# Query projections computed in row halves beside the gate and up products, and placed ahead of the weight folds

## The reference, cut to what matters

```python
xn = layernorm(x)
q  = xn @ Wq;  k, v = split(xn @ Wkv)
s  = softmax_causal(q @ k.T / 4) @ v @ Wo + bo
gate = xn @ gate_w.T + (xn @ gate_a.T) @ gate_b.T      # rank 16
up   = xn @ up_w.T   + (xn @ up_a.T) @ up_b.T
hidden = silu(gate) * up                                # 1376 wide
y = hidden @ down_w.T + (hidden @ down_a.T) @ down_b.T
out = x + s * silu(y)
```

## Time and profile before

| | |
|---|---|
| median of 3 runs | 969.41 us (967.91 to 973.47) |
| the profiled execution | 968.28 us, its span 966.6 us |
| granted clock of TensorE, mean | 0.98 |
| PE busy | 902.3 us, 93% of the span |
| DVE busy | 580.3 us, 60% |
| ACT busy | 490.9 us, 51% |
| POOL busy | 318.7 us, 33% |

### The profile page before, as it was taken

One profiled execution on the slowest core, in us unless ns is written; L12 is line 12 of the kernel. 1 busy time (PEld: TensorE's weight loads), 2 busy tenths in 40 slices (PEclk: granted clock), 3 DMA queues, 4 the chain that ended last, 5 costly groups with the idle time before them and its releaser, 6 DMA issues.

```text
span 966.6 us, 21098 instructions
## 1 busy us (share of the span) xinstructions
PE 902.3 (93%) x8075; PEld 633.4 (66%) x8075; DVE 580.3 (60%) x1681; ACT 490.9 (51%) x990; POOL 318.7 (33%) x320
## 2 busy tenths in 40 slices
PE   2797999999999999999999999998999999999996
PEld 2665666666666666767576666554777777777774
DVE  6755666666666666565756575767666667621134
ACT  2433555556565555555656565656454544545110
POOL 4022225252525252525252434441122213211036
PEclk8899999999999999999999999999899999999998
DMA  9466243333334242424243434347556566335644
GB/s 297 130 196 191 82 116 104 115 107 104 117 92 129 83 138 67 149 56 140 71 135 86 118 103 118 98 140 226 154 151 173 147 184 173 110 94 166 193 133 159
DMA packets 142946, 129.20 MB, mean 134 GB/s; under 512 B 36176, under 2 KB 104368, under 8 KB 142624
## 3 DMA queue, kind: packets, MB, share of 16 engines
q1 hardware_dynamic: 142848, 127.87, 44.6%
HBM read 74.07 MB, written 53.22 MB: 132 GB/s over the span
## 4 chain that ended last, share of the span: by engine, by line
PE 79%; DVE 8%; DMA 6%; ACT 2%; SPq 2%; issue 2%; POOL 0%; POOLq 0%; DVEq 0%; ACTq 0%
PE bank L965 25%; PE o L1134 12%; PE bank L999 12%; PE s L1098 9%; PE st L1117 7%; PE bank L267 3%; PE bank L269 2%; PE bank L268 2%; DVE junk L1624 2%; DVE neg_pad L1640 1%; PE bank L940 1%; PE bank L944 1%; DMA q<-scratch_q 1%; DVE hid L1489 1%; SPq L648 1%
## 5 line engine op out<-in xcount | busy, mean ns | idle before, releaser
L1380 ACT ACTIVATE prob<-st 128x512 f32<-128x512 f32 (+1 forms) x640 | 323.1, 554 | 258.4 <-PE st L1117 257.9
L1624 DVE CUSTOM_DVE_ANT_0 junk<-s,mask 128x128 bf16<-128x128 f32 (+3 forms) x512 | 229.3, 487 | 114.0 <-PE s L1098 113.4
L1627 DVE TENSOR_REDUCE part_max<-s 128x1 f32<-128x512 f32 x256 | 163.8, 681 | 97.0 <-PE s L1098 96.9
L1098 PE MATMUL s<-k,q 64*128 64x512 f32 (+3 forms) x768 | 150.9, 380 | 14.4 <-DVE part_max L1624 9.9
L533 POOL TENSOR_SCALAR_AFFINE_SELECT prob<-prob 128x512 f32<-128x512 f32 x128 | 82.7, 658 | 223.1 <-ACT prob L1380 222.6
L965 PE MATMUL bank<-x_hi,w_hi 64*128 64x512 f32 (+1 forms) x704 | 150.5, 415 | 2.4 <-DVE hid L1489 1.1
L1134 PE MATMUL o<-prob,v 128*32 128x512 f32 (+3 forms) x1536 | 143.7, 492 | 0.0
L965 PE MATMUL bank<-x_lo,w_hi 64*128 64x512 f32 (+1 forms) x704 | 142.6, 392 | 0.0
L965 PE MATMUL bank<-x_hi,w_lo 64*128 64x512 f32 (+1 forms) x704 | 141.6, 389 | 0.0
L1117 PE MATMUL st<-q,k 64*128 64x512 f32 (+3 forms) x768 | 130.0, 355 | 1.9 <-ACT prob L1380 1.8
L999 PE MATMUL bank<-down_hi,hid_in 64*128 64x256 f32 x1056 | 114.1, 289 | 0.3 <-DVE y L1505 0.3
(11 more groups left out here) (138 smaller groups left out, 1092.1 us busy)
## 6 DMA issues: line engine op xcount, KB each, us to landing
hid_in<-scratch_hid SPq DMA_DIRECT2D x16, 1408.0 KB, 7.1
q<-scratch_q SPq DMA_DIRECT2D x60, 200.0 KB
scratch_hid<-tanh_hid_hi SPq DMA_DIRECT2D x40, 256.0 KB, 2.1
scratch_hid<-hid_lo SPq DMA_DIRECT2D x40, 256.0 KB, 2.5
scratch_o<-o_sb SPq DMA_DIRECT2D x32, 256.0 KB
scratch_q<-proj_hi SPq DMA_DIRECT2D x30, 256.0 KB
k<-scratch_k SPq DMA_DIRECT2D x30, 192.0 KB
ctx<-scratch_o SPq DMA_DIRECT2D x16, 256.0 KB, 3.8
```

Of the source, the lines that this page charges most:

```text
L1098: pe.matmul(sb_[(p + odd) % S_BANKS][:, 0:wd], q[half, g % 2, h // 2, qt * P:(qt + 1) * P], k[half, g % 2, k0:k0 + wd], start=True, stop=T ...
L1380: nc.scalar.activation(prob[:, job % 3, h, 0:JOB_COLS[j]], st[at % ST_BANKS][:, 0:JOB_COLS[j]], ACT.Exp, scale=float(HD) ** -0.5).then_inc ...
L1624: ins = dve.tensor_tensor_reduce(junk[:, n % S_BANKS, 0:wd], bank_[:, 0:wd], mask[:, C - wd:C], 1.0, LOWEST, ALU.add, ALU.max, part[:, h, ...
L1627: ins = dve.tensor_reduce(part[:, h, qt, dst:dst + 1], bank_[:, 0:wd], AX.X, ALU.max)
```

## The change

Eleven of the 16 projections of queries (4 blocks of heads for 4 chunks of tokens), those inside the loop over `h` (`AFTER[1:]`, now `BESIDE_HIDDEN`), are computed by `changing_over` with the steps of the output product. The left 256 tokens of the chunk go to `bank[0]` and the right 256 to `bank[1]`. In the first two steps the upper 64 rows of the array add their part of the left tokens while the lower 64 rows add theirs of the right ones; then both change over. 12 matmuls of 128 rows by 512 columns become 48 of 64 rows by 256 columns. Such a projection takes both banks. ACT and DVE read it in two halves each. A new semaphore `p_left` counts the left half read by DVE, and `p_lo` the right one; whoever takes either bank next waits for both.

The second part is the order. The projection now stands directly behind `hidden(h, 1)` and ahead of the two folds, on all engines.

```diff
+BESIDE_HIDDEN = AFTER[1:]
@@ bank_order (and likewise in the loops of SP, PE, ACT and DVE)
             if c == 1:
+                yield "proj", *AFTER[SOON + h]
                 if h + 1 < NH:
                     for i in range(2):
                         yield "fold", h + 1, i
-                yield "proj", *AFTER[SOON + h]
@@ bank_places
-        if kind == "hidden" or kind == "down" and a < SPLIT_DOWN or kind == "out" and a < SPLIT_OUT:
+        if kind == "hidden" or kind == "proj" and (a, b) in BESIDE_HIDDEN or kind == "down" and a < SPLIT_DOWN or kind == "out" and a < SPLIT_OUT:
             used = (0, 1)
@@ read_out
+            if kind == "proj" and (a, b) in BESIDE_HIDDEN:
+                return (p_left, BESIDE_HIDDEN.index((a, b)) + 1), (p_lo, projection(a, b) + 1)
@@ project
+                if (c, blk) in BESIDE_HIDDEN:
+                    cols = slice(blk * P, (blk + 1) * P)
+                    yield from changing_over(
+                        ("proj", c, blk), lambda kt: [(wqh[:, kt, cols], xh[:, c, kt]), (wqh[:, kt, cols], xl[:, c, kt]),
+                                                      (wql[:, kt, cols], xh[:, c, kt])], OUT_STEPS)
+                    return
@@ split_projection (ACT)
-                nc.scalar.activation(projected(n)[0], bank_of(key)[:, :], ACT.Copy).then_inc(p_hi, 1)
+                if (c, blk) in BESIDE_HIDDEN:
+                    for i in range(2):
+                        ins = nc.scalar.activation(projected(n)[0][:, COLUMNS[i]], bank[i][:, COLUMNS[i]], ACT.Copy)
...
+                ins.then_inc(p_hi, 1)
@@ low_projection (DVE)
+                if (c, blk) in BESIDE_HIDDEN:
+                    for i, read in enumerate((p_left, p_lo)):
+                        dve.tensor_tensor(lo[:, COLUMNS[i]], bank[i][:, COLUMNS[i]], hi[:, COLUMNS[i]], ALU.subtract).then_inc(read, 1)
```

More of the change, by code:

```diff
@@ L396, in layer @@
         p_lo = sem("p_lo")
+        p_left = sem("p_left")
         p_stored = [sem(f"p_stored{i}") for i in range(2)]
@@ L759, in background @@
                         if c == 1:
+                            yield STEPS["proj"]
+                            store_projection(*AFTER[SOON + h])
                             if h + 1 < NH:
@@ L763, in background @@
                                     load_more_raw(2 * (h + 1) + i)
-                            yield STEPS["proj"]
-                            store_projection(*AFTER[SOON + h])
                 for h in range(NH):
@@ L1063, in background @@
                         if c == 1:
+                            yield from project(*AFTER[SOON + h])
                             if h + 1 < NH:
@@ L1066, in background @@
                                     yield from fold(h + 1, i)
-                            yield from project(*AFTER[SOON + h])
                 for h in range(NH):
@@ L1187, in split_projection @@
                     act.wait_ge(p_stored[n % 2], 3 * DMA * (n // 2))
-                nc.scalar.activation(projected(n)[0], bank_of(key)[:, :], ACT.Copy).then_inc(p_hi, 1)
+                if (c, blk) in BESIDE_HIDDEN:
+                    for i in range(2):
+                        ins = nc.scalar.activation(projected(n)[0][:, COLUMNS[i]], bank[i][:, COLUMNS[i]], ACT.Copy)
+                else:
+                    ins = nc.scalar.activation(projected(n)[0], bank_of(key)[:, :], ACT.Copy)
+                ins.then_inc(p_hi, 1)
             def copy_value(c):
@@ L1329, in background @@
                         if c == 1:
+                            yield STEPS["proj"]
+                            split_projection(*AFTER[SOON + h])
                             if h + 1 < NH:
@@ L1333, in background @@
                                     split_weight(h + 1, i)
-                            yield STEPS["proj"]
-                            split_projection(*AFTER[SOON + h])
                 for h in range(NH):
@@ L1456, in low_projection @@
                     dve.wait_ge(zero_stored, DMA * (B + 2))
-                dve.tensor_tensor(lo, bank_of(key)[:, :], hi, ALU.subtract).then_inc(p_lo, 1)
+                if (c, blk) in BESIDE_HIDDEN:
+                    for i, read in enumerate((p_left, p_lo)):
+                        dve.tensor_tensor(lo[:, COLUMNS[i]], bank[i][:, COLUMNS[i]], hi[:, COLUMNS[i]], ALU.subtract).then_inc(read, 1)
+                else:
+                    dve.tensor_tensor(lo, bank_of(key)[:, :], hi, ALU.subtract).then_inc(p_lo, 1)
             def low_of_low(n, part_, raw, at):
@@ L1574, in background @@
                         if c == 1:
+                            yield STEPS["proj"]
+                            low_projection(*AFTER[SOON + h])
                             if h + 1 < NH:
@@ L1578, in background @@
                                     low_weight(h + 1, i)
-                            yield STEPS["proj"]
-                            low_projection(*AFTER[SOON + h])
                 for h in range(NH):
```

## The result

| | before | changed |
|---|---|---|
| median of 12 runs | 970.00 us | 975.85 us |
| range | 967.88 to 973.47 | 973.81 to 977.17 |
| the profiled execution | 968.28 | 973.99 |
| its span | 966.6 | 971.2 |

The ratio is 1.0054 (95% interval 1.0039 to 1.0068): 0.5% slower, on the line between "no change" and "slower" that the prediction had drawn. The forecast was 971.5 and the range 961 to 980. The direction it leaned to was right, the size was less than half of what came. The profiled executions differ by 5.7 us and their spans by 4.6: before, 1.7 us lie around the span, after, 2.8.

The account below looks back on a forecast made before the run. PE was taken as the bound. A block: -1.09 + 1.21 + 0.20 = +0.32, ten blocks +3.2, the eleventh projection -0.6, together +2.6 on the profiled 968.28; forecast 971.5 us, range 961 to 980.

Parts of the forecast that it names:

- PE bounds, and nothing can absorb a new wait: Blocks from 125 to 632 us: PE waits only 4.7 us there, so any new wait costs in full.
- Shape changes: Per block, array switches between 64-row pairs and 128-row matmuls fall from twelve to seven, 0.2 each, some 1.0 us saved.
- The new matmuls: Projection's half-size pairs: 0.118 us each, 24 pairs 2.84 against 2.78 for the old matmuls, no gain by itself.
- The rival on weight loads: Projection pairs: serial weight loads would make a pair 0.21 us and the kernel about 996; no separate chance given.
- The change-over in the middle: Inside the projection, waiting for the second step to finish: costed at nothing, at most 0.1 us a block.
- The wait for the reading: First fold behind the projection: PE stalls 1.21 us a block while ACT and DVE read it; bounds 1.10 and 2.4.
- the waits of score pairs on maxima: Behind the first fold's stall, a score pair waits 0.2 us a block for DVE's wide maximum; zero to 0.5 possible.
- The eleventh projection: At h = 10, without folds: 5.98 us falls to 5.37, a gain of 0.6.
- The sum: Whole kernel: ten blocks at +0.32 give +3.2, -0.6 at h = 10, together +2.6 us.
- Rival 1: Projection's reading is hidden or much shorter: 957 us with no stall, 963 with half; chance 0.17 together.
- Rival 2: DVE becomes the bound behind the stall, PE waits again for a score bank: 980 us at 1.0 a block; chance 0.27.

Follow-up runs that it names:

- form alone: Kernel before with only the new half-size matmuls in both banks, projection still behind the folds: 974.14 us against 972.38, ratio 1.0029.
- order-alone run: Kernel before with only the projection moved ahead of the folds, its 12 matmuls of 128 rows kept: 975.43 us against 972.38, ratio 1.0036.
- late low part: Changed kernel with DVE's low part of the first fold put behind the two maxima: 975.39 us against 969.85 of before, ratio 1.0069.
- short reading: Changed kernel with ACT and DVE reading only 8 columns of each projection half: 967.50 us against 972.38 of before, ratio 0.9947.

## Why the prediction was right or wrong, point by point

- *PE bounds, and nothing can absorb a new wait*: right. The ten waits of 1.17 are in the time in full.
- *Shape changes*: forecast seven instead of twelve, each some 0.2. The sign was right, the count is not one that the rows give: between 64-row pairs and 128-row matmuls there are ten changes before; after, there are six, the one from the sum to the first pair included. The forecast didn't use the count, it added up the steps, and that sum holds: 9.12 less the stall of 1.25 and the 0.38 of the two score pairs is 7.49, 1.11 below the 8.60 of before, where 1.09 was forecast. That is a remainder; no run has the new block without any wait.
- *The new matmuls*: right to the hundredth. Six pairs took 0.80 and 0.71 (forecast 0.82, 0.71), twelve pairs 1.43 (1.44), 0.118 a pair. The rival on weight loads is refuted. The trace has 0.18 for one load of 128 columns, longer than the 0.118 of a whole pair with its two loads, so the loads must lie beside matmuls. At 126.28 both loads of the next pair start while the score pair of 126.27 is at work on both halves of the rows. The Trainium skill (TensorE: Matmul & The Clock Gate, LDWEIGHTS) puts a load of 128 columns at 128 / 1.2, an estimate of 107 ns; the trace differs, and the measurement decides. The rule that the prediction quotes beside it, that loads overlap matmuls only on other rows, is not borne out by the row at 126.28 either.
- *The change-over in the middle*: no wait in PE's list. The 0.25 from the 384-column score pair to the next L1009 is 0.08 over its columns. It goes with the late weight load of that pair and not with the semaphore: in the run with the form alone the change-over stands behind a score pair of 512 columns whose load did not wait (131.54), and the next L1009 follows at 131.78, the plain 0.23; and the pair with the late load at 134.16 has its 0.1 too, without any change-over behind it.
- *The wait for the reading*: 1.25 by my own count (the fold starts at 131.03, the score pair at 129.45, and 0.33 is their distance without a wait), forecast 1.21. ACT's 0.65 was 0.66, DVE's 0.75 was 0.76.
- *The step that was mis-sized*: the waits of score pairs on maxima. The prediction had one of them, 0.2 behind the stall; that one came (134.16 is 0.44 after 133.72, and the sum 0.43 after it, instead of 0.33 each: 0.2). It missed the other one, ahead of the stall. The step before it is shorter than in the old order (0.71 of pairs in place of a fold's step with two changes of shape), so the 384-column pair would start at 127.44, and its load ahead of that. But the load waits for the first of the two maxima that DVE had started at 126.70, and starts at 127.51. `st` and score pair together took 0.58 instead of 0.40. That 0.18, and 0.04 at the wait, are what turned +0.32 into +0.53 in this block, and +0.56 over ten. The order-alone run has such waits, and a loss of 0.27, without any wait at the fold. That DVE's place for the first low part makes the second one late was tested by itself (late low part, 0.20 a block); the first one is read from the rows and was not removed in any run.
- *The eleventh projection*: -0.40, forecast -0.6. Its wait was 1.17, as forecast (about 1.2). The missed 0.2 is the same as in the blocks: `st` and the 384-column pair took 0.57 there (629.21 to 629.78) instead of 0.40.
- *The sum*: ten blocks and the eleventh came to 5.6 - 0.4 = +5.2 by the trace, where +2.6 was forecast. So in the blocks the forecast's 3.2 became 5.6. The remaining 0.65 of the measured 5.85 I can't assign; the clock alone moves more from run to run. The range of 961 to 980 held easily, but it is wide: it would have held a result of the other sign too.
- *Rival 1* (hidden reading) is refuted by the 11.7 us; its price list was right in kind, as the short reading shows, but too generous by the 0.4 of the two score pairs a block. *Rival 2* (DVE as the next bound) was there in small: 0.38 a block in two score waits, short of the 0.4 at which I had let it decide, and together with the stall enough to bring the result to the edge of "slower".

## What to carry to other kernels

When a step is moved, lay out again what stood between it and the next user of its buffer: here 1.85 us of other work had hidden 1.6 us of reading, and moving the step took that cover away. The change paid off when a piece of that cover was moved along, and most when each half of the result was also released by itself. A cover that is moved is taken from somebody else: in two of the runs above the next reader's wait came up instead. And a step that gets shorter makes every consumer of a shared small buffer on the way (here three score banks) due earlier: list those waits on the weight-load row too, not only on the matmul row.

## What the runs showed of the hardware

- A score pair whose weight load had to wait is late twice by about 0.1: it starts 0.33 behind the 512-column pair before it instead of 0.23, although no shape changes, and what follows it is 0.08 to 0.1 late again (0.25 behind 384 columns instead of 0.17 at 127.79; at 134.59 0.43 instead of 0.33). Together that is the 0.2 that the load's row shows as its wait.
- Two half-width readings cost little more than one of full width: 0.66 for ACT against 0.60, 0.76 for DVE against 0.69. One half alone takes 0.38 and 0.42; the second one starts 0.28 and 0.34 behind the first, before that has ended. With 8 columns each they still cost 0.25 and 0.24 together.
- In the stretch from 650 to 725 us the granted clock fell to half (1.2 GHz) in each of the twelve profiles, in different places and for 3.4 to 17 us in all. For each 3.4 us at half the program lagged by 0.7 to 1.6 us, most at 706 to 720 us. Why it falls there is not shown; PE is busy for 61.5 of 68 us from 632 on, and for 500.9 of 507 in the blocks ahead, where the clock stays full. All twelve profiles also have half the clock for some microseconds before 102 and behind 847 us. It bounds what a single run can tell here.
